# A two-layer block on one core: the first batch's steps reordered, the last projection ahead, and token statistics on ScalarE in two passes

## What is computed

```
xn = layernorm(x)                                  # mean and variance of each token's 256 channels
x_, z = split(xn @ in_proj.T);  u = silu(conv(x_) + b)
dt, B, C = split(u @ x_proj.T); delta = softplus(dt @ dt_proj.T + dt_b)
h = exp(delta * A) * h + delta * B * u             # along 512 tokens, 512 channels x 16 states
y = ((h * C).sum(states) + u * D) * silu(z)
q = nearest fp6 value of xn / scale, times scale   # a scale for each block of 32 channels
out = x + y @ out_proj.T + q @ wq.T + bias
```

## Time and profile before

| | |
|---|---|
| median of three runs | 2140.81 us (2137.47 to 2140.95) |
| profiled execution, its own time | 2136.74 us |
| its span, first to last instruction | 2134.9 us |
| DVE busy | 1522.0 us, 71% |
| PE busy | 1675.0 us, 78% |
| ACT busy | 1009.9 us, 47% |
| POOL busy | 943.0 us, 44% |

### The profile page before, as it was taken

The page is one execution under the profiler, slowest core; times in us unless marked ns, Lnnn a source line. Parts: engine busy times, 40 slices in busy tenths (PEclk is TensorE's granted clock), DMA queues, the critical chain, the costliest instruction groups (busy, mean ns, idle before and its releaser), DMA issues.

```text
span 2134.9 us, 22187 instructions
## 1 busy us (share of the span) xinstructions
PE 1675.0 (78%) x6696; PEld 747.9 (35%) x6696; DVE 1522.0 (71%) x2256; ACT 1009.9 (47%) x1542; POOL 943.0 (44%) x676
## 2 busy tenths in 40 slices
PE   7399999999999999999364768687686959687355
PEld 7252626253443535262121224132232414133022
DVE  6446464646465564545217988999999999999995
ACT  3026253443435252525234564757576575757441
POOL 2700000000000000000238778988898898988761
PEclk9999989898989899898686879788797969788576
DMA  5563636344261536260314132433324232432410
GB/s 182 203 103 103 103 100 98 114 76 137 55 134 58 89 105 102 97 113 10 107 59 149 51 111 89 142 123 120 120 99 157 93 125 89 139 128 98 150 50 10
DMA packets 103060, 223.84 MB, mean 105 GB/s; under 512 B 12641, under 2 KB 64994, under 8 KB 99282
## 3 DMA queue, kind: packets, MB, share of 16 engines
q1 hardware_dynamic: 99922, 214.69, 36.2%
q0 software_dynamic: 3072, 8.37, 1.1%
HBM read 169.56 MB, written 53.48 MB: 104 GB/s over the span
## 4 chain that ended last, share of the span: by engine, by line
DVE 22%; PE 14%; issue 7%; POOL 4%; POOLq 2%; DMA 1%; DVEq 1%; ACT 1%; SPq 0%; ACTq 0%
DVE ps L1462 16%; PE ps L1555 6%; DVE work L1468 5%; POOL work L1198 3%; PE ps L1580 2%; PE ps L1587 2%; PE ps L1589 1%; PE ps L1563 1%; PE ps L1591 1%; PE ps L1590 1%; PE ps L1572 0%; POOLq L1246 0%; DVEq L1435 0%; POOLq L1168 0%; DVE xn_step L1442 0%
## 5 line engine op out<-in xcount | busy, mean ns | idle before, releaser
L1198 POOL TENSOR_TENSOR work<-rep,bc 128x1024 f32<-128x1024 f32 x256 | 600.3, 2366 | 116.8 <-PE ps L1580 85.6
L1462 DVE TENSOR_TENSOR_SCAN ps<-ps,work 128x512 f32<-128x512 f32 x512 | 623.5, 1218 | 37.5 <-POOL work L1198 27.5
L1338 ACT ACTIVATE ps<-rep,a_neg 128x512 f32<-128x512 f32 x512 | 345.3, 687 | 315.0 <-DVE work L1468 313.8
L713 DVE TENSOR_REDUCE m<-ps 128x1 f32<-128x512 f32 x512 | 328.2, 686 | 160.3 <-PE ps L819 157.6
L636 ACT ACTIVATE prob<-ps 128x1024 f32<-128x1024 f32 x256 | 257.4, 1022 | 225.7 <-PE ps L843 223.8
L1468 DVE TENSOR_TENSOR work<-ps,bc 128x512 f32<-128x512 f32 x512 | 343.9, 672 | 0.0
L1580 PE MATMUL ps<-work,pick 128*32 128x512 f32 x1024 | 186.1, 810 | 185.3 <-DVE work L1468 185.3
L577 POOL TENSOR_TENSOR m_parts<-m,nil 128x16 bf16<-128x16 f32 x32 | 7.1, 222 | 604.8 <-DVE m L713 604.8
L1555 PE MATMUL ps<-xn_t,in_taps 128*128 128x510 f32 (+3 forms) x512 | 241.3, 627 | 2.2 <-ACT xn_t L1268 1.5
L819 PE MATMUL ps<-k_st,q_st 96*128 96x512 bf16 x512 | 201.0, 437 | 31.2 <-DVE m L713 24.1
L843 PE MATMUL ps<-q_st,k_st 99*128 99x512 bf16 x512 | 166.9, 424 | 0.7
(11 more groups left out here) (176 smaller groups left out, 2058.6 us busy)
## 6 DMA issues: line engine op xcount, KB each, us to landing
rep<-rep_rows SPq DMA_DIRECT2D x128, 512.0 KB, 5.8
w<-in_w SPq DMA_DIRECT2D x32, 1024.0 KB
bc<-bc_rows SPq DMA_DIRECT2D x32, 512.0 KB, 4.7
rep_rows<-inputs SPq DMA_DIRECT2D x32, 512.0 KB, 5.4
qk_parts<-parts SPq DMA_DIRECT2D x96, 128.0 KB
q_st<-qk_parts SPq DMA_DIRECT2D x96, 128.0 KB, 10.5
k_st<-qk_parts SPq DMA_DIRECT2D x96, 128.0 KB, 11.4
dispatch<-zeros SPq DMA_DIRECT2D x4, 1280.0 KB, 10.5
```

What stands on the lines that cost most here:

```text
L713: nc.vector.tensor_reduce(m[:, g % 2, qt, 2 * pair + i:2 * pair + i + 1], ps[:, S0 + i, :], AX.X, ALU.max).then_inc(s_reduced, 1)
L1198: nc.gpsimd.tensor_tensor(work[:, n % WS, :, :], rep[:, g % RS, 2 * h:2 * h + 2, 1, :], bc[:, k, 0, :].unsqueeze(1).broadcast_to([P, 2, SE ...
L1338: nc.scalar.activation(state(m), rep[:, g % RS, 2 * h + i, 0, :], ACT.Exp, scale=a_neg[:, c, 2 * h + i, k:k + 1]).then_inc(decay_ready, 1)
L1462: nc.vector.tensor_tensor_scan(state(m), state(m), work[:, n % WS, i, :], 0.0, ALU.mult, ALU.add).then_inc(state_ready, 1)
```

## The change

1. **Ahead of the loop.** On DVE `statistics(0)` moves in front of `tap_weights`. POOL gathers, adds and takes the root for batch 1 before the loop; ACT weighs its rows, and normalises it, there; DVE has its statistics there too. ACT does `scale_step(0)` before the first `silu`, and the four silu(z) after `softplus(0)`; PE turns the quantised values (`turn`) before `project_bc(0)` and projects z after `project_dt(0)`. A one-element `Exp` stands in front of the loop. `LATE` is gone, so batch 1 has the same piece numbers as the others. The load of `rep` is waited for in two halves.
2. **In the loop.** The clamp L1445 goes. ACT does its lower side, as `over_one` (Relu(v - 1)) at piece 6, and `scale_step` puts the 1 back through its bias; the upper side is dropped. For batches 2 to 7 DVE's `statistics` and `aggregate` go. ACT does `sums` at -7 (a Copy with `accum_out`) and `squares` at -5 (Square of x less the mean, with `accum_out`), and POOL `means` at -3 makes the mean in between. `add_experts` goes from -5 to -6.
3. **The end.** Bias, quantised values, residual and the first two chunks' share of batch 7's projection are at pieces 20 to 23, the third chunk's at 28 to 31; behind the loop stands the fourth chunk's share alone. Every batch's output is stored in two halves.

```diff
-DVE_AT = {"max": 0, "binade": 4, "statistics": -7}
-POOL_AT = {"down": 6, "grid": 11, "up": 14, "gather": -15, "add": -5, "input": 26, "root": -1}
+DVE_AT = {"max": 0, "binade": 4}
+POOL_AT = {"down": 6, "grid": 11, "up": 14, "gather": -15, "add": -6, "means": -3, "input": 26, "root": -1}
-          "weigh": -10, "z": (23, 23, 25, 25), "silu_z": 26, "quant": (28, 28)}
+          "weigh": -10, "sums": -7, "squares": -5, "z": (23, 23, 25, 25), "silu_z": 26, "quant": (28, 28)}
...
+                def means(f):
+                    pool.wait_ge(sums_ready, f - 1)
+                    nc.gpsimd.tensor_scalar(moments[:, :, 0], moments[:, :, 0], 1.0 / DM, None, ALU.mult)
+                    pool.drain()
+                    nc.gpsimd.tensor_scalar(centre[:, :], moments[:, :, 0], -1.0, None, ALU.mult).then_inc(centre_ready, 1)
...
                 root(0)
+                pool.drain()
+                place_gather(1)
+                gather(1, range(TT))
                 scale_down(0)
                 for k in range(GRID_STEPS):
                     to_grid(0, k)
                 scale_up(0)
-                pool.drain()
-                place_gather(1)
-                gather(1, range(TT))
+                add_experts(1)
+                root(1)
...
+                def sums(f):
+                    act.wait_ge(x2_ready, f + 1)
+                    act.wait_ge(rstd_ready, f)
+                    for t in range(TT):
+                        r = nc.scalar.activation(e_rows[:, t, :], x2[:, f % XS, t, :], ACT.Copy, accum_out=moments[:, t, 0:1])
+                    r.then_inc(sums_ready, 1)
+
+                def squares(f):
+                    act.wait_ge(centre_ready, f - 1)
+                    act.drain()
+                    for t in range(TT):
+                        r = nc.scalar.activation(e_rows[:, t, :], x2[:, f % XS, t, :], ACT.Square, bias=centre[:, t:t + 1],
+                                                 accum_out=moments[:, t, 1:2])
+                    r.then_inc(moments_ready, 1)
...
+                def over_one(f):
+                    act.wait_ge(step_ready, f + 1)
...
+                    nc.scalar.activation(xn_step[:, :, :], xn_step[:, :, :], ACT.Relu, bias=shifts[:, 0:1])
...
-                    dve.drain()
-                    cross = xn_step[:, :, :].rearrange("p t c -> p (t c)").rearrange("p (c i) -> p i c", i=2)
-                    nc.vector.tensor_scalar(cross, cross, 1.0, 4.0, ALU.max, ALU.min).then_inc(step_ready, 1)
...
-                tap_weights()
-                dve.wait_ge(a_exp, 1)
...
                 statistics(0)
                 aggregate(0)
+                tap_weights()
...
                 quantise_weights()
+                statistics(1)
+                aggregate(1)
...
                 for t in range(TT):
-                    if t == 0:
-                        pe.wait_ge(out_copied, (BATCH - 1) * HALVES)
-                    out_proj(BATCH - 1, t, TB[t // 2])
+                    out_gated(BATCH - 1, t, TB[t // 2], range(3, DC))
```

More of the change, by code:

```diff
@@ L957, in mix_block @@
         eps = buf("eps", [P, TT])
+        shifts = buf("shifts", [P, 3])
+        idle = buf("idle", [P, 1])
         slot_cur = buf("slot_cur", [P, TT], I32)
@@ L1048, in chains @@
         def chains(n):
-            return [(f, n - (f - 1) * PIECES - (LATE if f == 1 else 0)) for f in range(1, BATCH)]
+            return [(f, n - (f - 1) * PIECES) for f in range(1, BATCH)]
         def state(m):
@@ L1202, in _ @@
                 nc.gpsimd.memset(eps[:, :], EPS)
+                for i, value in enumerate((-1.0, -2.0 ** -22, 1.5 * 2.0 ** 20)):
+                    nc.gpsimd.memset(shifts[:, i:i + 1], value)
+                nc.gpsimd.memset(idle[:, :], 0.0)
                 nc.gpsimd.memset(one_row[:, :], 1.0).then_inc(set_up, 1)
@@ L1349, in _ @@
                     copy_turned(0, k, k)
+                weigh_experts(1)
+                over_one(0)
+                scale_step(0)
                 for c in range(DC):
@@ L1353, in _ @@
                 e.then_inc(u_ready, 1)
-                for c in range(DC):
-                    act.wait_ge(z_done, c + 1)
-                    nc.scalar.activation(sz[:, 0, c, :], ps[:, Z_FIRST[c], :], ACT.Silu).then_inc(z_taken, 1)
+                for k in range(KD):
+                    copy_quant(0, k, k)
                 copy_rows(0, 2)
-                scale_step(0)
                 for c in range(DC):
@@ L1362, in _ @@
                 softplus(0)
+                for c in range(DC):
+                    act.wait_ge(z_done, c + 1)
+                    nc.scalar.activation(sz[:, 0, c, :], ps[:, Z_FIRST[c], :], ACT.Silu).then_inc(z_taken, 1)
+                act.wait_ge(w_turned, 1)
+                nc.scalar.activation(fw_t[:, :, :], ps[:, W_FIRST, :].rearrange("p (k d) -> p k d", d=DM), ACT.Copy).then_inc(w_copied, 1)
+                normalise(1)
                 act.wait_ge(a_ready, 1)
+                nc.scalar.activation(idle[:, :], idle[:, :], ACT.Exp)
+                act.drain()
                 for n in range(BATCH * PIECES):
@@ L1366, in _ @@
                     decay(b, q)
-                    if n == FIRST_ACT["w"]:
-                        act.wait_ge(w_turned, 1)
-                        nc.scalar.activation(fw_t[:, :, :], ps[:, TB[0], :].rearrange("p (k d) -> p k d", d=DM), ACT.Copy).then_inc(w_copied, 1)
-                    for k in range(KD):
-                        if n == FIRST_ACT["quant"][k]:
-                            copy_quant(0, k, TB[1 - k])
-                    if n == FIRST_ACT["weigh"]:
-                        weigh_experts(1)
                     for h in range(HALVES):
@@ L1378, in _ @@
                     for f, at in chains(n):
-                        if f > 1 and at == ACT_AT["weigh"]:
+                        if at == ACT_AT["weigh"]:
                             weigh_experts(f)
+                        if at == ACT_AT["sums"]:
+                            sums(f)
+                        if at == ACT_AT["squares"]:
+                            squares(f)
                         if at == ACT_AT["normalise"]:
@@ L1610, in _ @@
                     in_proj_taps(2 + c, c, range(TAPS), in_done)
-                for c in range(DC):
-                    in_proj(Z_FIRST[c], c, z_done)
+                pe.wait_ge(quant_ready, 1)
+                for k in range(KD):
+                    turn(k, k, quant_turned)
                 project_bc(0, 2)
@@ L1616, in _ @@
                     project_dt(0, c, DT_FIRST[c])
+                pe.wait_ge(quant_copied, KD)
+                for c in range(DC):
+                    in_proj(Z_FIRST[c], c, z_done)
+                turn_weights()
                 pe.wait_ge(diag_ready, 1)
@@ L1643, in _ @@
                             out_proj(b - 1, t, TB[t // 2])
+                    for t in range(TT):
+                        if b == BATCH - 1 and q == LAST_OUT[t]:
+                            if t == 0:
+                                pe.wait_ge(out_copied, b * HALVES)
+                            pe.wait_ge(y_ready, b * DC + 2)
+                            if t % 2 == 0:
+                                out_bias(TB[t // 2])
+                            out_known(b, t, TB[t // 2])
+                            out_gated(b, t, TB[t // 2], range(2))
+                        if b == BATCH - 1 and q == LAST_GATED[t]:
+                            pe.wait_ge(y_ready, b * DC + 3)
+                            out_gated(b, t, TB[t // 2], range(2, 3))
                     for f, at in chains(n):
```

123 lines of the change are left out of this document (64 added, 59 removed).

## The result

The changed kernel took 2081.57 us (median of four runs, 2081.09 to 2083.93), against 2139.92 us (2137.47 to 2140.95, four runs) for the kernel before on the same chip: **ratio 0.9731, 95% interval 0.9714 to 0.9748**. Forecast were 2077 us and a range from 2059 to 2094. The profiled execution took 2081.49 us, its span is 2079.7; 55.2 us of span are gone, where 61.2 were forecast. Of all executions in this document two were far slower than the rest (one of the kernel before, 3276 us, and one of e9, 3938 us); no ratio and no median given here contains them.

| | before | after | gain | forecast |
|---|---|---|---|---|
| to the first scan | 1133.4 | 1115.1 | 18.3 | 20.0 |
| first scan to last `gate_y` | 979.0 | 956.9 | 22.1 | 26.3 |
| from there to the end | 22.6 | 7.7 | 14.9 | 14.9 |

A forecast was written before the change was run, and what follows sets the result against it. DVE was taken to bound the loop, a chain over all engines the start, PE's projection the end. Gains 20.0 + 26.3 + 14.9 = 61.2 us off the profiled 2136.74 gave 2075.5, stated as 2077; range 2059 to 2094.

The forecast's parts named there:

- The start, 20.0 forecast: Ahead of the loop: the shortened chain over all engines brings the first scan to 1113.4 from 1133.38 us.
- Now the statistics come first: Ahead of the loop: `statistics(0)` before `tap_weights` on DVE makes everything up to `normalise` 4.67 us earlier.
- The halves of the load: First drive: two of four operand blocks suffice, so it starts at 1111.0, not 1113.8; start gain 17.2 without this.
- The wait at `squares`: Loop, piece 28, batches 0 to 5: ACT waits for POOL's `means`, so DVE waits 3.3 us a batch, 19.8 in all.
- The rival without a wait: Loop: POOL runs 3 us or more ahead, the centre comes in time; 19.8 us more gain, 2057; chance 0.16.
- Statistics and aggregate: Loop, DVE: moving them off gains 1.75 us a batch in batches 0 to 5.
- The clamp, 2.0 a batch: Loop, DVE: removing the clamp gains 2.0 us a batch; only 0.7 if the mask is held up each time.
- The rival of the mask held up: Loop: POOL always holds up the mask, 9 us less gain; part of the dearer-sides rival, 2093, chance 0.27.
- Batches 0 and 1: Loop: without batch 1's late steps they become steady, from 130.7 and 132.9 to 120.05 us each; 22.5 gained.
- The end, 14.9 and 14.9: Behind the last scan: four matmuls in two passes remain, at 3.0 us; 14.9 us gained, 14.1 to 16.8.
- ACT's new work: Loop, ACT: `sums`, `squares` and `over_one` add 4.8 us a batch; `accum_out` nothing to some 0.25 us each.
- the slower rival: Loop: costly `accum_out` makes ACT the bound; 2153 us at 2.0 us each; chance 0.03.

The follow-up runs named there:

- e9: Changed kernel with POOL's `means` one piece earlier and `tap_weights` behind batch 0's root: 2063.30 us, ratio 0.965 to the kernel before.
- e5: Changed kernel with DVE's `tap_weights` waiting until POOL's root for batch 0 is done: 2080.66 us, ratio 0.9742 to the kernel before.
- e4: Changed kernel with the two halves of the operand load (`rep`) waited for together again: 2084.78 us, ratio 0.9761 to the kernel before.
- e1: Changed kernel with POOL's `means` one piece earlier, ahead of the fourth `scale_input`: 2063.05 us, ratio 0.9668 to the kernel before.
- e2: Changed kernel with statistics of batches 2 to 7 back on DVE, without `sums`, `means` and `squares`: 2072.24 us, ratio 0.971 to the kernel before.
- e3: Changed kernel with both sides of the clamp back on DVE behind the mask, ACT's `over_one` gone: 2083.55 us, ratio 0.9769 to the kernel before.
- e10: Changed kernel with `means` one piece earlier and the clamp back on DVE: 2069.63 us, ratio 0.9683 to the kernel before.
- e7: Changed kernel with batch 1's steps from its first convolution on five pieces late again: 2095.35 us, ratio 0.9812 to the kernel before.

## Why the prediction was right, and where it was not

- **The start, 20.0 forecast, 18.3 measured.** The chain went as written. The step that was off is "Now the statistics come first: everything up to `normalise` is 4.67 us earlier": the gain at `normalise` was 2.4 (1050.19 to 1047.78), because `tap_weights`, moved behind the statistics, now ran beside POOL's root, and slowed it by 1.9 us (e5); another 0.3 us is a longer gap inside the root (0.81 instead of 0.49 us, in e5 too). The Trainium skill's lock (SBUF — State Buffer, "SBUF: two separate sides"), which I had weighed for the mask alone, bears on this place too: by it one of the two engines waits for a whole instruction of the other. The trace agrees: POOL's two operations of 1.1 us stand beside multiplies of 1.19 to 1.22 us, and each ends 0.06 us behind the end of one. I counted what moved on DVE and not what would then be next to it. The halves of the load were worth 3.5, not 2.8 (e4). POOL's quantisation was through at 1070.5, 2.5 us earlier than I allowed: cover enough.
- **The wait at `squares`, +3.3 forecast.** Measured +3.4 a batch, 20.5 in all by e1 against 19.8: the place, the two engines and the size were right. The rival without a wait didn't come about by itself; e1 makes it, by one number in a table.
- **Statistics and aggregate, 1.75 a batch.** Pieces 16 to 27 give 1.65, and e2 takes them back.
- **The clamp, 2.0 a batch: the term that was mis-sized.** At its own piece it is 1.9 (13.6 over seven, e3). In the loop it is worth 3.9 (e3) or 5.2 (e10) in seven batches, 0.6 to 0.7 each. The sentence "what is taken from DVE is gained if nothing else then makes it wait" was not followed up for pieces 0 to 16. I read PE's 90.52 of 120 us busy as slack, and called DVE the bound from the first scan to the last. PE's work isn't spread evenly; the trace of before already had this row, for pieces 1 to 16 of batch 2:

```profile
1401.80:1458.30 56.50, 56.50 (x196) 26.37 (x196) 56.26 (x66) 28.06 (x40) 44.99 (x23) 0.98 0.27 96
```

  So behind DVE's 2.0 stood PE, at once, and piece 16 already waited for it (1.24 us behind `project_bc`, as in after). The rival of the mask held up would have brought a similar sum for another reason, but the mask did not take over the clamp's hold-up: its seven in the loop take 13.3 us in after, 13.6 in e3 and 13.6 in the kernel before. Only in batches 2, 4 and 6 was the clamp the short one, as the rival had it for all. Against the kernel before, the steady batches won 1.6 us at piece 4 and lost 0.5 at pieces 10 to 15: 1.1 where I had 2.0. And even this 1.1 is not the clamp's: e3, with the clamp on DVE, is 0.9 under before in this stretch. It is PE's own work there that became shorter, a term that the forecast didn't have. From the sum to the end of `project_bc` PE takes 57.8 us in batch 3 of before and 56.6 in batch 2 of after, both at a mean clock of 0.97; the matmuls of the output projection, which now sets the bias first and for two token blocks at once, take 14.6 of them instead of 15.8. This is read from the traces; no run isolates it.
- **Batches 0 and 1, 22.5 forecast, 23.2 measured** (263.7 to 240.5 us); e7 shows `LATE` to be nearly half of it. That the sum came so near is in part luck: 120.05 us each was the base, and they took 118.7 and 121.8.
- **The end, 14.9 and 14.9.** The matmuls took 3.78, not 3.0; the last store, left out at "at most 0.8", gave the same back: from the start of the last copy to the last instruction 3.2 us instead of 4.0. So the 14.9 is right by two misses that cancel.
- **ACT's new work.** `accum_out` cost 0.09 us each, 0.4 for four, between the lower price (nothing) and the upper one (0.25); the slower rival did not come about. The Relu took 1.14 us where I had 1.04, without effect.

The forecast of 61.2 was 6.0 too high: 1.7 at the start, 4.2 in the loop. The loop's miss is batches 2 to 5, where 1.8 were forecast as gain and 2.6 were lost; pieces 0 to 16, where the clamp's 2.0 a batch was forecast, make 3.4 of these 4.4.

## What to carry to other kernels

Work that goes to an idle engine is gained only if its operands come in time: look at what stands ahead of each small producer in its engine's queue, since moving one such producer a piece earlier was worth 20 us here, more than the work that had been moved (9.4). Before counting what is taken from the bounding engine, look for stretches in which another engine has no gap either, by windows of half a batch and not of a whole one. And when two operations change places on one engine, ask what each then runs beside on the others.
